# Thirteen of the hundred sign operations of L2 are made by GpSimd instead of ScalarE

## The reference, cut to what matters

```python
s_src = features @ a_src
s_dst = features @ a_dst
e = leaky_relu(s_src[src] + s_dst[dst], negative_slope=0.01)
ee = exp(e - segment_max(e, dst)[dst])
alpha = ee / segment_sum(ee, dst)[dst]
h = segment_sum(alpha[:, None] * features[src], dst)
return elu(h)
```

## Time and profile before

| what | value |
|---|---|
| time, median of 3 runs | 1907.07 us (1906.61 to 1913.65) |
| span of the profiled execution | 2674.2 us; no separate time is given for it |
| busy in that span | PE 1501.4, DVE 1423.4, ACT 1008.8, POOL 1227.4 us |
| L2's aggregation in it | 1668.3 to about 1790 us |
| steps of span 0, 1, 2, 3 begin | 1671.0, 1703.8, 1728.6, 1751.9 us |

### The profile page before, as it was taken

How to read it: one execution, slowest core, us unless ns; L and a number is a source line. 1 busy time by engine, 2 the same in 40 slices (tenths; PEclk the granted TensorE clock), 3 DMA queues, 4 the chain that set the end, 5 groups by cost and what they waited for, 6 DMA issues and landing times. The chain is left out here.

```text
span 2674.2 us, 43621 instructions
## 1 busy us (share of the span) xinstructions
PE 1501.4 (56%) x12903; PEld 1250.3 (47%) x12903; DVE 1423.4 (53%) x3785; ACT 1008.8 (38%) x2221; POOL 1227.4 (46%) x1328
## 2 busy tenths in 40 slices
PE   3555555555555654555555774754134656555795
PEld 2444444434444443344434673753033645444785
DVE  6455555555555554555555787871023534434685
ACT  3333333333333333333333651750003534434683
POOL 2555555555555554545553460546724343444100
PEclk7677777777777767777777787885556777777897
DMA  5222222222222222222221210022201111111100
GB/s 116 54 58 56 58 59 57 59 57 61 57 58 60 56 59 52 60 55 58 59 57 35 62 59 3 2 87 34 35 17 33 37 34 37 32 41 33 40 26 14
DMA packets 125233, 128.69 MB, mean 48 GB/s; under 512 B 80959, under 2 KB 88435, under 8 KB 124840
## 3 DMA queue, kind: packets, MB, share of 16 engines
q0 software_dynamic: 35776, 62.74, 10.4%
q1 hardware_dynamic: 63778, 57.41, 7.8%
q10 hardware_dynamic: 25542, 6.81, 1.1%
HBM read 116.64 MB, written 10.20 MB: 47 GB/s over the span
## 5 line engine op out<-in xcount | busy, mean ns | idle before, releaser
L634 POOL DMA_INDIRECT shared<-kv_tab,idx x784 | 763.2, 974 | 674.3 <-DMA idx<-in_src 459.3
L836 PE MATMUL bank<-key_hot,lo_hot 128*128 128x350 f16 x784 | 220.8, 394 | 586.5 <-DVE count L698 392.4
L836 PEld LDWEIGHTS bank<-key_hot,lo_hot 128*128 128x128 f16 x784 | 59.3, 101 | 703.4 <-issue 690.4
L2282 POOL DMA_INDIRECT count<-att_tab,count x240 | 228.3, 951 | 301.7 <-PE bank L2827 193.4
L698 DVE TENSOR_TENSOR count<-count,bank 128x350 f32 x392 | 205.4, 524 | 109.4 <-issue 73.6
L735 DVE TENSOR_TENSOR acc<-acc,bank 65x64 f32 x98 | 21.3, 217 | 429.2 <-remote 425.8
L779 ACT ACTIVATE expo<-score 128x32 f32<-128x32 f32 x98 | 22.5, 229 | 587.3 <-DVE score L716 566.9
L769 ACT ACTIVATE lo_dist<-iota_neg,tile_lo 128x128 f16<-128x128 f32 x784 | 238.5, 389 | 0.0
L2656 ACT ACTIVATE shared<-shared 128x126 f32<-128x126 bf16 x336 | 144.4, 484 | 172.0 <-PE bank L2804 88.6
L683 DVE TENSOR_SCALAR key_hot<-iota_key,tile_key 128x350 f16<-128x350 f16 x784 | 193.3, 319 | 0.0
L851 PEld LDWEIGHTS bank<-hots,msg 128*65 128x65 f32 x1568 | 183.8, 221 | 0.4 <-DVE msg L725 0.4
(11 more groups left out here) (528 smaller groups left out, 3237.8 us busy)
## 6 DMA issues: line engine op xcount, KB each, us to landing
shared<-in_edge_attr SPq DMA_DIRECT2D x97, 256.0 KB
shared<-lo_tab SPq DMA_DIRECT2D x28, 512.0 KB
shared<-kv_tab,idx POOLq DMA_INDIRECT x784
count<-att_tab,count POOLq DMA_INDIRECT x240
qwin<-q_tab ACTq DMA_DIRECT2D x196, 16.0 KB
kv_tab<-count SPq DMA_DIRECT2D x1, 1600.0 KB, 10.4
idx<-in_src SPq DMA_DIRECT2D x97, 4.0 KB, 1.6
g_edge<-att_tab,count POOLq DMA_INDIRECT x94
```

Source lines behind the costliest of these rows:

```text
L634: nc.gpsimd.indirect_dma_start(kv[:, s, c, :], None, kv_tab, bass.IndirectOffsetOnAxis(ap=idx[:, s, c:c + 1], axis=0)).then_inc(kv_in[s], 16)
L836: last = nc.tensor.matmul(bank[6 + q % 2][:, 0:KC], lo_hot[:, c, :], key_hot[:, c, :], start=i == 0, stop=i == GT - 1)
L2282: nc.gpsimd.indirect_dma_start(ring[s][:, j, 0:D + 2], None, att_tab[1], bass.IndirectOffsetOnAxis(ap=src_i[:, t:t + 1], axis=0)).then_inc ...
```

## The change

GpSimd gets a sign buffer of its own, `pool_signs`, one row of bytes for one step, and makes the signs of the steps in `BY_POOL`: h = 9, 13, 17 and 21 in span 0, h = 15, 18 and 21 in each of spans 1 to 3. It computes `(ad_row < -u) * -1`, so its bytes are -1 or 0 where ScalarE's are -1 or +1. ScalarE skips those steps, and its four buffers go round over the 87 others. VectorE's AND takes the bytes from one or the other buffer and waits on that maker's semaphore. Five semaphores are allocated in another way and cleared with the rest.

```diff
+        pool_signs_f = sb("pool_signs", [P, MS // 4])
+        pool_signs, pool_signs_i = pool_signs_f[:, :].bitcast(i8), pool_signs_f[:, :].bitcast(i32)
         steps = [(k, h) for k in range(len(SPANS)) for h in range(NT)]
+        BY_POOL = [n for n, (k, h) in enumerate(steps) if h in ((9, 13, 17, 21) if k == 0 else (15, 18, 21))]
+        pool_order = {n: i for i, n in enumerate(BY_POOL)}
+        act_order = {n: i for i, n in enumerate(n for n in range(len(steps)) if n not in pool_order)}
...
+        signed_p, sign_free_p = short_sem("d_signed_by_pool"), short_sem("d_pool_sign_used")
...
-                        dve.wait_ge(signed, n + 1)
-                        dve.wait_ge(mask_free, n + 1)
-                        nc.vector.tensor_tensor(masks_i[:, n % MR, 1, 0:width], signs_i[:, n % SR, 0:width], kind, ALU.bitwise_and).then_inc(sign_free, 1)
+                        if n in pool_order:
+                            dve.wait_ge(signed_p, pool_order[n] + 1)
+                            dve.wait_ge(mask_free, n + 1)
+                            nc.vector.tensor_tensor(masks_i[:, n % MR, 1, 0:width], pool_signs_i[:, 0:width], kind, ALU.bitwise_and).then_inc(sign_free_p, 1)
+                        else:
+                            i = act_order[n]
+                            dve.wait_ge(signed, i + 1)
+                            dve.wait_ge(mask_free, n + 1)
+                            nc.vector.tensor_tensor(masks_i[:, n % MR, 1, 0:width], signs_i[:, i % SR, 0:width], kind, ALU.bitwise_and).then_inc(sign_free, 1)
...
+                    def signs_by_pool(k):
+
+                        cols = slice(SPANS[k][0] * P, (SPANS[k][-1] + 1) * P)
+                        for n in BY_POOL:
+                            if steps[n][0] == k:
+                                h = steps[n][1]
+                                if pool_order[n] > 0:
+                                    pool.wait_ge(sign_free_p, pool_order[n])
+                                nc.gpsimd.tensor_scalar(pool_signs[:, 0:len(SPANS[k]) * P], ad_row[:, cols], u_neg[:, h:h + 1], -1.0, ALU.is_lt, ALU.mult).then_inc(signed_p, 1)
+
                     pool.drain()
+                    signs_by_pool(0)
                     for k, ts in enumerate(SPANS[:-1]):
...
+                        signs_by_pool(k + 1)
                         pool.wait_ge(shared_ok, k + 1)
...
-                        if n >= SR:
-                            act.wait_ge(sign_free, n - SR + 1)
-
-                        nc.scalar.activation(signs[:, n % SR, 0:len(ts) * P], ad_row[:, cols], ACT.Sign, bias=u_col[:, h:h + 1]).then_inc(signed, 1)
+                        if n in pool_order:
+                            continue
+                        i = act_order[n]
+                        if i >= SR:
+                            act.wait_ge(sign_free, i - SR + 1)
+
+                        nc.scalar.activation(signs[:, i % SR, 0:len(ts) * P], ad_row[:, cols], ACT.Sign, bias=u_col[:, h:h + 1]).then_inc(signed, 1)
```

More of the change, by code:

```diff
@@ L1709, in build @@
         diag = work_diag = ctx.enter_context(nc.sbuf_tensor("diag", [P, 2, MT, P], fp32))
-        limits_ok, limits_moved, dg_ok, dg_rep, dg_out = (sem(f"d_{n}") for n in ("limits", "limits_moved", "diag", "diag_rep", "diag_out"))
+        limits_ok, limits_moved, dg_ok, dg_rep, dg_out = (short_sem(f"d_{n}") for n in ("limits", "limits_moved", "diag", "diag_rep", "diag_out"))
         with nc.Block() as block:
@@ L1806, in build @@
         signs_i = signs_f.bitcast(i32).rearrange("p (r n) -> p r n", r=SR)
+        pool_signs_f = sb("pool_signs", [P, MS // 4])
+        pool_signs, pool_signs_i = pool_signs_f[:, :].bitcast(i8), pool_signs_f[:, :].bitcast(i32)
         steps = [(k, h) for k in range(len(SPANS)) for h in range(NT)]
+        BY_POOL = [n for n, (k, h) in enumerate(steps) if h in ((9, 13, 17, 21) if k == 0 else (15, 18, 21))]
+        pool_order = {n: i for i, n in enumerate(BY_POOL)}
+        act_order = {n: i for i, n in enumerate(n for n in range(len(steps)) if n not in pool_order)}
         general = lambda eng: eng.If(apart(eng) > 0)
         nc.clear_and_free_semaphores([t_ready, t_in, t_edges, t_rows, t_ea, t_marks, f_in, f_out, f_rep, f_e2n, ea_up, ea_down, t_stored, t_start, t_made, t_kept,
-                                      x_ok, agg_ok, agg_used, worst, worst_t, gl_in, gl_ok, gl_used, gl_done, scaled])
+                                      x_ok, agg_ok, agg_used, worst, worst_t, gl_in, gl_ok, gl_used, gl_done, scaled,
+                                      limits_ok, limits_moved, dg_ok, dg_rep, dg_out])
+        signed_p, sign_free_p = short_sem("d_signed_by_pool"), short_sem("d_pool_sign_used")
         big = count[:, :, :].rearrange("p h n -> p (h n)").bitcast(fp32)
```

## The result

The changed kernel takes 1932.85 us (median of 4 runs, 1932.11 to 1938.24), the kernel before in the same rounds 1910.36 us: 22.5 us more. The ratio of the runs is 1.011, interval 1.0084 to 1.0135. Slower, as forecast, by 1.1% where 1.1% was forecast. In microseconds it is 22.5 where 20.3 were forecast; the median itself lies 5.4 us above the forecast 1927.4, and 3.3 of these come from the kernel before, which took 1907.07 us when the forecast was made.

The account below looks back on a forecast made before the run. VectorE's chain of steps was taken to bound the L2 aggregation stage. Terms 2.5 + 6.3 + 5.6 + 5.6 + 0.3 = +20.3 us on 1907.07 gave 1927.4 us (+1.1%), range 1911 to 1942.

Parts of the forecast that it names:

- Who paces: In the aggregation of L2, VectorE's chain of steps is the stage's time; ScalarE waits 15.4 us for VectorE.
- the relief: Taking 13 signs (11.5 us) off ScalarE returns at most 0.5 us, at the end of span 0.
- Price of a sign: On GpSimd, 2.75 us for 768 columns and 3.05 us for 896; ends 2.2 and 4.6 / 5.2 us.
- the waits at h=15: VectorE idles at this AND in spans 1 to 3 for GpSimd's sign: about 5.7, 4.1 and 4.1 us.
- the tail: GpSimd's last four operations start behind the sign of h=21 and make VectorE late: +0.3 us.
- Stretches: A GpSimd sign blocks VectorE once, by 0.64 us for 768 columns or 0.75 us for 896.
- Span 0: Seven tiles: four blocks of 0.75 us less 0.5 us, signs otherwise in time: +2.5 us.
- Spans 1 to 3: Signs queued behind GpSimd's tile combining stall VectorE: +6.3 us in span 1, +5.6 us each in spans 2 and 3.
- TensorE's clock: Clock sinks after each stall, costed at nothing; rival: 1.2 GHz until the eviction, 7 us, 1934 us, chance 0.04.
- GpSimd in time: Rival: in timed runs the sign of h=15 is ready or nearly so; only blocks remain, +7.5 us, 1914.6; chance 0.17.
- ScalarE as the pacer: Rival: ScalarE paces the timed runs, up to 11.5 us could come back, 1895.6 us; chance 0.05.
- the lock: Rival: VectorE stands for the whole sign of 2.75 or 3.05 us, 22 us more than the blocks, 1948; chance 0.05.

Follow-up runs that it names:

- the kernel without the 13 signs: Against the kernel before, nobody makes GpSimd's 13 signs; VectorE reads a buffer cleared once, ScalarE makes 87: timed +0.6 us, ratio 1.0003.
- the shared evictions: Against the kernel before, signs unchanged, ScalarE takes the last three evictions of each span (9 of 19) from VectorE: timed -2.3 us, ratio 0.9995.
- two buffers: Against the change, GpSimd's sign buffer has two rows used in turn: timed +22.4 us to the kernel before.
- the unused signs: Against the kernel before, ScalarE still makes all 100 signs; GpSimd also makes its 13, which nobody reads: timed +19.8 us.
- the kernel with four signs in span 0: Against the change, GpSimd makes only h=9, 13, 17 and 21 of span 0: timed +11.7 us to the kernel before, ratio 1.0052.
- the four narrow ones: Against the kernel before, ScalarE makes all signs; GpSimd adds four unused sign operations in span 0, each 4 columns wide: timed +1.0 us.
- the repeated kernel: GpSimd making only the four signs of span 0, measured once more unchanged: timed +4.4 us to the kernel before, ratio 1.0029.

## Why the prediction was right, point by point

**Who paces.** VectorE, as read from ScalarE's 15.4 us of waits. That ScalarE isn't the pacer is shown by the kernel without the 13 signs (-0.1 us), that VectorE is by the shared evictions (-2.3 us). The 0.5 us that I gave the relief was there in the change, at the end of span 0: from the AND of h=21 to the first eviction it takes 5.32 us (1299.48 to 1304.80) against 5.76 before (from the row at 1700.45, below). In the kernel without the 13 signs the same part takes 5.56 us, and VectorE then waits 0.16 us for TensorE at the eviction.

**Price of a sign.** Taken as 2.75 and 3.05 us from L1234 plus a second operation; measured 3.02 and 3.48 with VectorE working beside it, 2.86 with VectorE standing still. This term was too small by 0.1 to 0.4 us, and it is a good part of the 2.3 us between 20.3 and 22.6: the waits at h=15 were 5.92, 4.34 and 4.35 us where I had 5.7, 4.1 and 4.1, those at h=18 0.60 instead of 0.35, and the tail 0.77 instead of 0.3. That is 1.9 us more together, and span 0 has another 0.8; the stretches in spans 1 to 3 came out some 0.6 below. The first sign is only 0.1 us dearer than I took it, so the dearer signs explain 0.3 of the 0.7 us at h=15; the rest stays open. How near the price came was partly luck: no row had this operation, and my ends reached from 2.2 to 5.2 us.

**Stretches.** 0.75 us for 896 columns and 0.64 for 768; measured 0.72 (1.11 - 0.39) and 0.61 (0.97 - 0.36), for one AND under a sign:

```profile
1288.31 1.11 DVE L1997 TENSOR_TENSOR acc<-diag,count 128x224 int32<-128x224 int32 x1
...
1322.86 0.97 DVE L1997 TENSOR_TENSOR acc<-diag,count 128x192 int32<-128x192 int32 x1
```

The Trainium skill (SBUF — State Buffer, "Who interferes with whom") calls the contention for the port pair that VectorE and GpSimd share an exclusive lock. Read as a block for the whole sign it doesn't fit these rows either: the AND was held up 0.7 of 3.5 us. Only the copy of 12 columns under the next point ends when the sign does, as a lock would have it.

**Span 0.** +2.5 forecast, +3.3 measured. I had GpSimd's period at 3.5 us against VectorE's 3.9. With 3.48 for the sign and 0.52 from its end to the next sign's start, with VectorE's AND between, it is 4.0 us, and VectorE's steps followed it: 1287.47, 1291.48, 1295.48, 1299.48. The single buffer was the pacer there after all, by 0.1 us a sign; with two buffers the steps lie 3.92 and 3.91 us apart. And the first sign cost more than one stretch. It runs from 1279.36 to 1282.66, and two operations of VectorE last longer beside it, an XOR (0.39 us before) and a copy of 12 columns (0.17 before), which ends when the sign does:

```profile
1279.51 1.10 DVE L1999 TENSOR_TENSOR acc<-acc,count 128x224 int32<-128x224 int32 x1
...
1282.18 0.51 DVE L1938 COPY tab<-dense 128x12 f32<-128x12 f32 x1
```

The sum: 1.2 us up to the AND of h=9, three periods of 4.0 instead of 3.16 us, less 0.4 of relief behind h=21, counted from this row of before:

```profile
1700.45 0.38 DVE L1984 TENSOR_TENSOR acc<-diag,count 128x224 int32<-128x224 int32 x1
```

**Spans 1 to 3.** +6.3, +5.6, +5.6 forecast, with 0.3 for the tail; +6.95, +6.25, +6.2 measured, the last with the tail. The wait at the tail was 0.77 us, since GpSimd's last operations start only when the dearer sign of h=21 ends.

**TensorE's clock.** As forecast it fell to 1.2 GHz (a granted 0.50 from 1321 on), after TensorE had idled from 1318 in VectorE's wait; it was back at 1.00 by 1328. Columns as in the earlier trace rows:

```profile
1321.00:1322.00 1.00, 0.00 (x0) 0.00 (x0) 0.00 (x0) 0.00 (x0) 1.00 (x1) 0.50 0.00 0
1326.00:1327.00 1.00, 1.00 (x12) 1.00 (x10) 0.94 (x2) 0.00 (x0) 0.94 (x1) 0.50 0.00 0
1329.00:1330.00 1.00, 1.00 (x19) 0.85 (x15) 1.00 (x2) 0.78 (x1) 0.99 (x2) 1.00 0.00 0
```

VectorE's waits hold none for TensorE at a mask or an eviction, so it cost nothing, as costed.

**The rivals.** The profile at the length of the timed runs shows the full waits at h=15 (5.92, 4.34, 4.35 us), so "GpSimd in time" with its +7.5 us is out; a sign takes 2.9 to 3.5 us, not 4.6 to 5.2; ScalarE as the pacer, the lock and the clock are answered above.

**What I had not seen.** That GpSimd's own later work is a price of its own, beyond the tail that I had costed at 0.3 us. In the change it was nearly hidden, because VectorE was already late from waiting for the signs; the unused signs laid it bare with 13.9 us of waits.

## What to carry to other kernels

Before moving work off an engine, look at what that engine waits for: if it waits for the engine you hope to speed up, the relief is worth little. Work put into another engine's in-order queue costs at the place where it stands: ask for each piece when its queue gets there and when the consumer does, and what now stands behind it. Here the same operation cost 0.4 us where it was wanted seven steps later, and 4.3 to 5.9 us of waiting where it was wanted before its turn.

## What the runs showed of the hardware

A GpSimd comparison with a second operation into bytes takes 3.9 ns per column (3.02 us for 768, 3.48 us for 896), three and a half times ScalarE's price for the same sign (0.85 us), while VectorE, reading two SBUF tensors, is held up only for about 0.8 ns per column that GpSimd reads, 0.6 to 0.7 us (0.97 us instead of 0.36, 1.11 instead of 0.39).

The part behind the stage isn't the same in all programs, though its instructions are. From VectorE's last multiply to L3's first indirect load it takes 26.1 and 25.9 us in the two executions of the kernel with four signs in span 0, 25.9 with the four narrow ones, and 22.9 in the changed kernel, 23.1 without the 13 signs. From the same multiply to the end it is 528.4 and 527.3, 524.3, and 521.6 and 517.3 us. In the other six changed kernels it is 519.2 to 522.0 us; the one with shared evictions has the long way to the first load (25.8 us) and no long last layer (519.2), so the two don't go together. That 528 came again in the repeated kernel speaks for a property of the program. Against it stand the repeated timed runs (+4.4 us after +11.7), and that the part ahead of the stage, alike in all these kernels, also lasts from 1261.6 to 1268.6 us, 1263.6 and 1261.9 in the two executions of the repeated one. Single executions can't settle it. What it is stays open; no experiment here tells the place of instructions in memory from other reasons, and that it is part of the timed differences that the stage doesn't explain is likely, not shown.
